# Values unsplit, a ring of six exponentials, and a new order and new banks on TensorE in a two-layer cross-attention

## The reference, cut to what matters

```python
q = (x @ Wq) -> [b, 20, 512, 16];  k, v = (ctx @ Wk), (ctx @ Wv) -> [b, 20, 1024, 16]
scores = q @ k.T / sqrt(16)
probs = softmax(scores)          # over the 1024 keys, with the maximum taken away
out = probs @ v                  # [b, 512, 320]
return out @ Wo + bo + x
```

## Time and profile before

| what | us |
| --- | --- |
| time, median of 3 runs | 323.3 (323.12 to 323.32) |
| span of the profiled execution, first to last instruction | 320.5 |
| before the steps | 0 to 109.2 |
| the 80 steps | 109.2 to 312.5 |
| after the steps | 312.5 to 320.5 |
| busy in the span: PE, DVE, ACT, POOL | 308.1, 259.9, 228.9, 77.8 |

### The profile page before, as it was taken

How to read it: one execution, slowest core, us unless ns; L and a number is a source line. 1 busy time by engine, 2 the same in 40 slices (tenths; PEclk the granted TensorE clock), 3 DMA queues, 4 the chain that set the end, 5 groups by cost and what they waited for, 6 DMA issues and landing times.

```text
span 320.5 us, 6083 instructions
## 1 busy us (share of the span) xinstructions
PE 308.1 (96%) x2086; PEld 166.4 (52%) x2086; DVE 259.9 (81%) x456; ACT 228.9 (71%) x468; POOL 77.8 (24%) x97
## 2 busy tenths in 40 slices
PE   7999999999999999999999999999999999999995
PEld 6678888876766634333344343334433453443335
DVE  1469899889986899998999899998999988893213
ACT  3556456543445797889878988888898877878982
POOL 6055157360434310010013100130441016101030
PEclk9999999999999999999999999999999999999999
DMA  7960007859946831471723817329065010110102
GB/s 228 322 200 0 2 2 199 246 142 179 225 127 204 183 80 54 95 107 52 125 60 76 126 42 124 75 68 125 27 124 92 37 50 30 57 33 26 38 30 83
DMA packets 20193, 32.79 MB, mean 102 GB/s; under 512 B 5539, under 2 KB 9667, under 8 KB 20163
## 3 DMA queue, kind: packets, MB, share of 16 engines
q1 hardware_dynamic: 19075, 31.27, 42.2%
q10 hardware_dynamic: 1088, 1.14, 1.2%
HBM read 20.63 MB, written 11.61 MB: 101 GB/s over the span
## 4 chain that ended last, share of the span: by engine, by line
PE 72%; ACT 9%; DVE 7%; issue 4%; DMA 4%; SPq 3%; POOL 1%; ACTq 0%; POOLq 0%; DVEq 0%
PE ps L1393 19%; PE ps L1370 13%; PE ps L1381 13%; PE ps L1221 10%; PE ps L1042 8%; ACT probs L701 4%; SPq L347 2%; ACT probs_last L701 2%; DVE mx L906 2%; PE ps L1108 2%; DMA QS<-mT 1%; DMA rec_rows<-recs 1%; PE ps L1168 1%; PE ps L1148 1%; DMA QS<-q_parts 1%
## 5 line engine op out<-in xcount | busy, mean ns | idle before, releaser
L906 DVE TENSOR_REDUCE mx<-ps 128x1 f32<-128x512 f32 x298 | 186.1, 683 | 16.3 <-PE ps L1370 14.6
L701 ACT ACTIVATE probs<-ps 128x512 f32<-128x512 f32 x216 | 113.5, 610 | 22.2 <-PE ps L1381 20.9
L1370 PE MATMUL ps<-KS,QS 48*128 48x512 f32 x256 | 77.9, 450 | 2.2 <-ACT probs L701 1.2
L1381 PE MATMUL ps<-QS,KS 50*128 50x512 f32 x256 | 72.1, 440 | 1.6 <-DMA QS<-mT 0.4
L1393 PE MATMUL ps<-probs,VS 128*32 128x512 f32 (+1 forms) x552 | 60.3, 511 | 0.3 <-ACT probs L701 0.3
L701 ACT ACTIVATE probs_last<-ps 128x512 f32<-128x512 f32 x104 | 54.8, 611 | 6.7 <-PE ps L1381 6.2
L1370 PEld LDWEIGHTS ps<-KS,QS 48*128 48x128 f32 x256 | 35.0, 184 | 36.8 <-DVE mx L906 16.2
L1381 PEld LDWEIGHTS ps<-QS,KS 50*128 50x128 f32 x256 | 33.9, 184 | 33.3 <-ACT probs L701 13.5
L1393 PE MATMUL ps<-probs_last,VS 128*32 128x512 f32 (+1 forms) x256 | 29.0, 524 | 0.0
L507 POOL CAST neg_p<-neg 128x16 fp32r<-128x16 f32 x10 | 2.1, 211 | 110.0 <-DVE neg L916 104.3
L683 ACT CAST parts<-ps 128x512 fp32r<-128x512 f32 (+1 forms) x18 | 10.5, 584 | 19.6 <-PE ps L1221 19.4
(11 more groups left out here) (186 smaller groups left out, 440.5 us busy)
## 6 DMA issues: line engine op xcount, KB each, us to landing
KS<-k_parts SPq DMA_DIRECT2D x48, 128.0 KB, 4.7
k_parts<-parts SPq DMA_DIRECT2D x8, 512.0 KB, 3.5
QS<-q_parts SPq DMA_DIRECT2D x48, 64.0 KB, 5.0
raw_rows<-o_raw SPq DMA_DIRECT2D x9, 256.0 KB, 2.0
q_parts<-parts SPq DMA_DIRECT2D x4, 512.0 KB, 3.9
cs<-in_ctx_dram SPq DMA_DIRECT2D x2, 768.0 KB, 9.3
KS_last<-k_parts SPq DMA_DIRECT2D x12, 128.0 KB, 4.6
xs<-in_x_dram SPq DMA_DIRECT2D x2, 640.0 KB, 6.3
```

What stands on the lines that cost most here:

```text
L701: act.activation(probs[t % 3][:, h, :], ps[:, bank_of["s", m], :], ACT.Exp, scale=float(D1) ** -0.5).then_inc(exp_done, 1)
L906: dve.tensor_reduce(mx[:, g % BUF, u:u + 1], ps[:, bank_of["m", n], :], AX.X, ALU.max).then_inc(max_done, 1)
L1370: pe.matmul(ps[:, bank, :], QS[g % BUF][rows, pair, qt * P:(qt + 1) * P], KS[g % BUF][rows, pair, half * 512:half * 512 + 512], start=True ...
L1381: pe.matmul(ps[:, bank, :], KS[g % BUF][rows, h // 2, kt * P:(kt + 1) * P], QS[g % BUF][rows, h // 2, :], start=True, stop=True).then_inc( ...
```

## The change

- `PLAN` and `BANKS` are new for all 80 steps. No values are in halves; `a` and `b` are gone. Some steps have no `v` and some have two. `EARLY` and `TAIL` are as before.
- Six steps of exponentials are kept instead of three (`RING`). The three new ones (`probs_more`) lie over the weights of layer two, q of layer one and the context of the second batch, which nothing reads once the projections are done; the exponentials of step 3 wait for that.
- The exponentials wait for the values of six steps ago, once a step instead of at every head.
- A step can have several extras. `X_LEAVES` names the exponential behind which ScalarE takes each extra away. The transpose of group 6 moves from step 45 to 46, that of group 9 from 69 to 70, and of the four `finC` one from 72 to 74, one from 74 to 75 and one from 79 to 77.
- What split a chain of matmuls in parts (`chain_part`) is gone; no chain was split before.

```diff
+    RING = 6
...
-    X_AT = {4: ("neg", 1), 11: ("neg", 2), 21: ("neg", 3), 29: ("neg", 4), 36: ("neg", 5), 45: ("neg", 6), 53: ("neg", 7), 57: ("fin", 0),
-            59: ("fin", 1), 61: ("neg", 8), 62: ("fin", 2), 69: ("neg", 9), 70: ("fin", 3), 72: ("finC", 4), 74: ("finC", 5),
-            77: ("finC", 6), 79: ("finC", 7)}
-    X_AFTER = {4: 3, 11: 2, 21: 1, 29: 2, 36: 2, 53: 2, 57: 3, 61: 2, 62: 2, 69: 3, 70: 2, 72: 3, 74: 1, 79: 3}
+    X_AT = {4: [("neg", 1)], 11: [("neg", 2)], 21: [("neg", 3)], 29: [("neg", 4)], 36: [("neg", 5)], 46: [("neg", 6)], 53: [("neg", 7)], 57:
+            [("fin", 0)], 59: [("fin", 1)], 61: [("neg", 8)], 62: [("fin", 2)], 70: [("neg", 9), ("fin", 3)], 74: [("finC", 4)], 75: [("finC",
+            5)], 77: [("finC", 6), ("finC", 7)]}
+    X_LEAVES = {18: [("neg", 1)], 45: [("neg", 2)], 84: [("neg", 3)], 117: [("neg", 4)], 145: [("neg", 5)], 183: [("neg", 6)], 213: [("neg", 7)],
+                230: [("fin", 0)], 239: [("fin", 1)], 245: [("neg", 8)], 249: [("fin", 2)]}
...
-    PLAN = ["m1mmm203vmm", "201m3v", "1mm2m03vm", "m21m03v", "m21m0max3mmb", "m10mamm23bmm", "01mm2m3v", "3m210mmab", "10mmm32mmv",
-            "m23m10mv", "m3m2mam01b", "m13mm2xam0mb", "10m3m2mv", "mmm1203vm", "0m312mvmm", "30m1am2b", "31m2mmm0mmv", "m0m21m3v",
-            "m2m301mv", "1m03m2mvm", "0m1am2mm3b", "mm01mxam23mb", "0m1mm23v", "mm10m3am2b", "m3mm12m0v", "3m10mm2mab", "mmm3120v",
-            "m32mm01v", "12mmm03v", "2m0x1mm3mv", "m1mm0am32mb", "0mm2m13mv", "1m3mm0mm2v", "m03ma2m1mmb", "12mm30vmm", "m301a2mb",
-            "mm01a3mxm2mb", "m0123mmv", "m3mm120v", "0m3m2mv1", "m201m3mmv", "m3m1m2mm0v", "mm1230mvm", "1m2m03v", "0m123mmv",
-            "mm3m102ammxb", "0m1mm32mv", "0mm12ma3mb", "0mm2m13mmv", "mm12a3mm0b", "30m1mmm2v", "2m10m3mv", "m203mm1mvm", "03mm2x1mv",
-            "0mma12m3mb", "m2m3m01mv", "m0m23m1mv", "2mm10mxm3v", "2m1ma0mm3b", "2mmm10xm3mmv", "m1m320mv", "mm31m2ax0mb", "1mmm0xm23mv",
-            "2m301mmv", "m10m32mmmv", "m03m21mv", "m3102mmv", "2mm1a0mm3b", "mm1320mv", "3210vx", "3210xv", "0132v", "3012xv", "0123v",
-            "1203x", "v1023v", "2130v", "0132xv", "0231v", "xv"]
+    PLAN = ["mm2m103", "132mmv0m", "12mmmm0vm3", "2m03v1m", "m32m1mmvx0", "12m0mmmvmm3", "21mmvmm30", "2mvm3m0m1v", "m2m013m", "1mm0mvm2mm3",
+            "32v1m0", "1mmvmm32m0xvm", "0132mmvm", "2mm013mmv", "3mm21mv0m", "m23m10", "mv2m3m0mmv1m", "m3m21m0", "mv2m1m3mm0v", "m1023m",
+            "mvm02m31m", "3mxv2m1m0mmv", "mmm201v3", "mm2m013m", "mvmmm210v3", "m21m0mm3", "0m32mv1m", "12mmv0mmm3", "2vmm1mm03v",
+            "mm031mvxm2", "mm3mm20m1v", "301mm2", "mv2mm30mm1", "m0m2mmvm31", "2v0m13mm", "m01v2m3", "m0mv3mmm21xv", "1mm30m2v", "m0132mmv",
+            "0m3m1m2v", "m1m023mm", "2m3v10m", "01mvm23m", "2m0vm1m3mm", "23mm0vmm1", "m21vm03", "0mmxvm123mmmvm", "31m0mm2vm", "1mm320mmvm",
+            "m302mv1m", "0m31mm2", "3mm0m2m1vm", "m23m1vm0m", "1m02vx3mmm", "m32vmm01m", "3vm01mm2v", "3m10m2mv", "0m1m2mxmm3m", "32vmmm01",
+            "0vmm3m2mx1mm", "2mvm1m0mv3", "m12mmmvx3mm0", "1mxm2mm03v", "m120mm3v", "m0mm213vm", "31mm0m2", "21m0v3", "2m10mmv3m",
+            "1mm2mv3mm0", "23v10", "1230xvvx", "1032v", "3120", "12v03", "30vx12", "30xv21", "01v32", "13xx20", "0132vvvv", ""]
+    BANKS = ["5021375", "4203175", "341207531", "425071", "435207134", "5207314053", "27140352", "71450237", "1542073", "5124037154", "20734",
...
         probs.append(sb("probs_last", [P, GH, SQ]))
-        wk1h, wk1l, wv1h, wv1l = (sb(name, [P, 2, DM]) for name in ("wk1h", "wk1l", "wv1h", "wv1l"))
-        wq1h, wq1l = (sb(name, [P, 3, DM]) for name in ("wq1h", "wq1l"))
-        q0T1 = sb("q0T1", [P, 3, SQ])
-        cs1 = sb("cs1", [P, NKT, DC])
+        wk1h, wk1l, wv1h, wv1l, wq1h, wq1l, q0T1, cs1 = passing(
+            ("wk1h", [P, 2, DM]), ("wk1l", [P, 2, DM]), ("wv1h", [P, 2, DM]), ("wv1l", [P, 2, DM]),
+            ("wq1h", [P, 3, DM]), ("wq1l", [P, 3, DM]), ("q0T1", [P, 3, SQ]), ("cs1", [P, NKT, DC]))
+        late = sb("probs_more", [P, (RING - 3) * GH, SQ])
+        sb("rest_of_projections", [P, 8 * DM + 6 * DM + 3 * SQ + NKT * DC - (RING - 3) * GH * SQ])
         k0bd, U, pT = passing(("k0bd", [P, 3, B, 3 * KEY0]), ("U", [P, B, 3, DM]), ("pT", [P, 2, COL0]))
...
+        probs += [late[:, n * GH:(n + 1) * GH, :] for n in range(RING - 3)]
...
                 act.wait_ge(s_mm, m + 1)
-                if t >= 3:
-                    act.wait_ge(pv_mm, t - 2)
-                act.activation(probs[t % 3][:, h, :], ps[:, bank_of["s", m], :], ACT.Exp, scale=float(D1) ** -0.5).then_inc(exp_done, 1)
+                if t >= RING and m % GH == 0:
+                    act.wait_ge(pv_mm, t - RING + 1)
+                if m == 3 * GH:
+                    act.wait_ge(proj_mm, len(order))
+                act.activation(probs[t % RING][:, h, :], ps[:, bank_of["s", m], :], ACT.Exp, scale=float(D1) ** -0.5).then_inc(exp_done, 1)
...
-                    if h == X_AFTER.get(t, GH) - 1 and t in X_AT and t == X_STEPS[X_AT[t]][-1]:
-                        leave(X_AT[t])
+                    for u in X_LEAVES.get(GH * t + h, ()):
+                        leave(u)
...
-            def chain_part(dst, pairs, s, part, parts_in):
-
-                for n in range(len(pairs) * part // parts_in, len(pairs) * (part + 1) // parts_in):
-                    m = pe.matmul(dst, *pairs[n], start=(n == 0), stop=(n == len(pairs) - 1))
-                if part == parts_in - 1:
-                    m.then_inc(s, 1)
...
-                                  probs[t % 3][:, h, cols], start=(kt == 0), stop=(kt == NKT - 1 and half != 0))
+                                  probs[t % RING][:, h, cols], start=(kt == 0), stop=(kt == NKT - 1 and half != 0))
...
-                        at = X_STEPS[X_AT[t]]
-                        unit(X_AT[t], *((at.index(t), len(at)) if len(at) > 1 else ()))
+                        unit(next(extras))
```

## The result

The changed kernel took 326.9 us (median of 4 runs, 324.5 to 328.4) against 323.3: a ratio of 1.0097, interval 1.0049 to 1.0145. Timed again later beside other kernels it took 324.9 us (12 runs, 321.5 to 326.5), ratio 1.0022 (0.9993 to 1.0051). So it is between no slower and 1% slower, and its runs lie far apart where those of the kernel before lie close; 319.6 was forecast, and neither median is near it. Ratios leave out runs more than 1.5% above the fastest of their kernel, here those in which TensorE's clock fell most, so for the changed kernel and its variants they are kinder than the medians (324.9 beside 323.5 us is 1.004, not 1.0022).

The account below looks back on a forecast made before the run. TensorE was taken to bound the kernel (busy 96%), VectorE and ScalarE close behind. No halves -3.2, fewer runs -5.0 and waits +4.5 make -3.7 us: from 323.3 to 319.6 us, range 314.3 to 324.4.

Parts of the forecast that it names:

- TensorE's work, -8.2 us: In the steps: no halves of values, -3.2 us, and fewer, longer stretches of scores and maxima, -5.0 us; 181.0 us left.
- the order does not pair values: In the order's strings: 74 of 80 values stand alone, though the description speaks of two steps' values back to back.
- Waits for banks, +4.5 us (18.6 in all): In the steps: TensorE waits for banks that VectorE or ScalarE empties late, 18.6 us instead of 14.1.
- a rule that does not carry: In the steps: waits are 1.28 times the surplus of reductions and exponentials over TensorE's time; 14.5 x 1.28 = 18.6 us.
- 199.6 was forecast: Sign: the steps, from first scores behind the early order to last values, take about 199.6 us instead of 203.3.
- transposes of maxima: First scores of a group wait for rows from SyncE's queue: between 0 and +2 us, taken as 0.
- Rival 1: In the steps: TensorE alone paces and waits stay at 14.1 us; 315.1 us, chance 0.22.
- Rival 2: In the steps: long stretches of scores and maxima fill the banks, +10.3 - 8.2 = +2.1 us; 325.4 us, chance 0.18.
- Rival 3: In the steps: VectorE was the bound already, every freed microsecond becomes a wait for a reduction; 323.3 us, chance 0.10.
- Waits of 2 us or more at the first scores of a group: Sign that the forecast is wrong altogether: such waits come from the DMA of the maxima.
- The sign for the waits: In the steps: longest waits in the runs of steps 8, 24, 29, 32, 49 to 50; VectorE's idle time falls some 4 us.

Follow-up runs that it names:

- the mended kernel: Changed kernel with SyncE's queue sending rows of maxima ahead of reciprocals: 317.8 us, 0.9835; with step 50's values also moved into a long run: 317.3 us, 0.9812.
- the filled kernel: Changed kernel with four and eight matmuls added where the first scores of groups 4 and 5 wait for rows of maxima: 325.8 us, 1.002.

## Why the prediction was wrong

- *TensorE's work, -8.2 us: right by the profile.* Single values still take 1.00 us and runs 0.19 plus 0.235 for a slot; by this tally the changed order is 180.8 us of work. That the order does not pair values, as it is called, held too.
- *Waits for banks, +4.5 us (18.6 in all): the right sign, too large, by a rule that does not carry.* With the queue mended the steps take 198.7 us, 17.9 above the tally, and 199.6 was forecast. But some 2 us of the 17.9 are the one spell of low clock (an estimate: 0.011 of clock at 0.2 us for 0.001), which leaves about 16, or +2. For the old order unsplit the same rule gives 15.8 x 1.28 = 20.2 us, and 25.9 were measured. So it is 3 us too high here and 6 us too low there, and no law; that the steps came near to 199.6 is luck. Why the old order lost so much is not settled; that its banks were laid out for halves is a guess that no run tests.
- *The step that failed: transposes of maxima, "between 0 and +2 us, I take 0".* I had the kind of place, and counted 3 to 3.5 us of slack at groups 4, 6, 7 and 9, but took only the row's own flight and not what stood in the queue ahead of it. The reciprocals' waits of 5.5 us at group 4 and 5.8 us at group 5 did; group 5, with 5.4 us between transpose and scores, was not on my list and had the longest stop. Two stops of 1.10 and 1.83 us in the profiled run, others in other runs, and with them the clock. At a full clock the changed kernel is near 320.9 us and the mended one near 316.2, by lines through their runs: some 4.7 us are the stops themselves and what they hold up.
- *What was missing altogether: the clock.* I read 1.00 in every window of before as a fact of the chip. Mean 0.979 in 16 runs costs the changed kernel about 4 us by the line through them (320.9 to 325.1 us). It explains about half of the 2 us between its two medians, whose runs had 0.975 and 0.980 in the mean. Put together, as an estimate: 319.6 less some 2.5 for waits, 4.7 for stops and 4 for the clock give about 326, where 324.9 and 326.9 were measured.
- *The rivals.* Rival 1 (315.1 us) is what the mended kernel comes near to, 317.3 to 317.8 us with the queue's own gain (1.4 us in the old order) in it. Rival 2 (long runs fill the banks, 325.4) had a number near the result by the wrong road: the run of twenty lost 2.3 us (2.0 where the clock stayed up), but breaking it gained nothing that can be told, and mending the queue with all long runs in place gained 1.9% (0.9835 against 1.0022). Rival 3 is out: the same VectorE work fits into steps of 198.7 us.
- *What I said would show it.* "Waits of 2 us or more at the first scores of a group" was listed as the sign of a wrong forecast, and it was the right sign: the longest wait of a weight load for them is 2.7 us in the profile. The sign for the waits failed: VectorE's idle time before reductions did not fall by 4 us from its 11.3 but rose to 16.6 in the changed kernel, and was 10.8 in the mended one.

## What to carry to other kernels

When an order of work becomes tighter, look at every transfer that has to land inside it with all that its queue does ahead of it, waits on landings above all: here each wait for a small write that had large loads ahead of it in the same queue delayed whatever came next by 4 to 6 us. Time several executions and look at the granted clock of each: a kernel near the limit of TensorE that lets it stand for 2 us can pay again for a spell at half clock. Splitting work can be right even where it costs TensorE more, perhaps because it parts long runs of matmuls whose results others must take away: test that part alone before dropping it.

## What the hardware showed that I had not expected

- One stop of 2.80 us, made on purpose in an otherwise unchanged kernel, lowered the clock in five of six runs (spell of 3.4 us in the profile); one of 0.67 us in none of twelve. In between, in single profiles of the changed kernel and its variants, the clock fell within 2 us of the end of every stop of 1.31 us or more (1.31, 1.33, 1.83, 1.88, 2.05 and 2.62 us), and at none of 1.03 to 1.20 us (six of them). Five more falls at the start of the steps, three in the run of twenty (in five profiles that have it, and in none of the three where it is broken) and one at 194.7 us in the filled kernel had no stop of 0.5 us just ahead. These are single executions: they don't give a length of stop that is safe.
- The kernel before is not free of it: of 63 runs beside the experiments, 7 had a clock of 0.989 or less and took 326.2 to 331.3 us.
- The same small write of reciprocals (128 partitions, 16 float32 each) took 4.1 us in the middle and 4.8 at most from issue to landing in the kernel before, 4.6 and up to 5.8 us in the changed kernel's profile, up to 6.4 us in its repetition, so the stop behind it changes from run to run. In the mended kernel, where it stands behind the rows of maxima and no longer right behind the twelve loads of the next stacks, it took 1.5 us in the middle. So the 4 to 6 us are not the write's own; that they are the loads' is read from this order alone.
